# Row maxima and row scales of seven blocks moved from TensorE transposes to 32 by 32 VectorE transposes

## The reference

```python
scale = cond @ norm_w.T + 1.0
ms = jnp.mean(x * x, axis=-1, keepdims=True)
h = x * (scale[:, None, :] * jax.lax.rsqrt(ms + EPS))
u = h @ up_w.T
val, gate = jnp.split(u, 2, axis=-1)
h = val * jax.nn.gelu(gate, approximate=False)
# act_quant: s = 127 / clip(max|h| over the row, 1e-5); round(h * s) / s
# weight_quant: s = 1 / clip(mean|w|, 1e-5); clip(round(w * s), -1, 1) / s
y = act_quant(h) @ weight_quant(down_w).T
return y + x
```

## Time and profile before

| | |
|---|---|
| median of 3 runs | 760.05 us (759.47 to 760.5) |
| profiled execution, own time | 759.19 us |
| its span, first to last instruction | 757.4 us |
| TensorE matmul busy | 737.0 us, 97% |
| VectorE busy | 546.7 us, 72%, 1066 instructions |
| ScalarE busy | 345.7 us, 46% |
| GpSimd busy | 98.9 us, 13%, all in the first third |
| TensorE clock granted | 0.999 |

### The profile page before, as it was taken

How to read it: one execution, slowest core, us unless ns; L and a number is a source line. 1 busy time by engine, 2 the same in 40 slices (tenths; PEclk the granted TensorE clock), 3 DMA queues, 4 the chain that set the end, 5 groups by cost and what they waited for, 6 DMA issues and landing times.

```text
span 757.4 us, 15715 instructions
## 1 busy us (share of the span) xinstructions
PE 737.0 (97%) x6218; PEld 610.5 (81%) x6218; DVE 546.7 (72%) x1066; ACT 345.7 (46%) x674; POOL 98.9 (13%) x137
## 2 busy tenths in 40 slices
PE   3999999999999999999999999999999999999998
PEld 2888889888578887888778887788878887688864
DVE  5467777888788775878667775777758776377747
ACT  5789756443254432553235442444325342233425
POOL 2211376763413000000000000000000000000000
PEclk9999999999999999999999999999999999999999
DMA  9877673756645444343533434343443333453302
GB/s 324 285 259 241 189 264 123 229 178 223 200 135 183 153 153 148 116 140 99 183 117 116 130 116 163 108 152 122 125 160 103 98 98 117 128 170 98 103 29 84
DMA packets 43929, 116.63 MB, mean 154 GB/s; under 512 B 4944, under 2 KB 5200, under 8 KB 42704
## 3 DMA queue, kind: packets, MB, share of 16 engines
q1 hardware_dynamic: 43856, 115.63, 47.6%
HBM read 98.83 MB, written 16.78 MB: 153 GB/s over the span
## 4 chain that ended last, share of the span: by engine, by line
PE 86%; DVE 5%; ACT 3%; issue 3%; DMA 1%; POOL 0%; SPq 0%; DVEq 0%; ACTq 0%
PE ps_v L525 16%; PE ps_v L526 15%; PE ps_v L527 15%; PE ps_y L626 12%; PE ps_g L526 8%; PE ps_g L525 8%; PE ps_g L527 8%; PE ps_v L690 1%; DMA sums<-in_up_t_dram 1%; DMA h<-in_x_rows_dram 1%; ACT g L733 1%; ACT w_hi L776 1%; DVE h L1053 0%; PE ps_m L609 0%; DVE xt L1004 0%
## 5 line engine op out<-in xcount | busy, mean ns | idle before, releaser
L525 PE MATMUL ps_v<-x_hi,w_hi 128*128 128x256 f16 x1216 | 332.0, 273 | 3.3 <-DVE ps_g L1036 1.3
L527 PE MATMUL ps_v<-x_hi,w_lo 128*128 128x256 f16 x1216 | 331.9, 273 | 0.0
L526 PE MATMUL ps_v<-x_lo,w_hi 128*128 128x256 f16 x1216 | 331.9, 273 | 0.0
L526 PE MATMUL ps_g<-x_lo,w_hi 128*128 128x256 f16 x640 | 174.8, 273 | 0.0
L527 PE MATMUL ps_g<-x_hi,w_lo 128*128 128x256 f16 x640 | 174.8, 273 | 0.0
L525 PE MATMUL ps_g<-x_hi,w_hi 128*128 128x256 f16 x640 | 174.8, 273 | 0.0
L715 ACT COPY ps_g<-ps_v 128x256 f32<-128x256 f32 x96 | 34.3, 357 | 230.7 <-PE ps_v L527 230.7
L525 PEld LDWEIGHTS ps_v<-x_hi,w_hi 128*128 128x128 f16 x1216 | 119.1, 98 | 21.4 <-DVE ps_g L1036 2.7
L526 PEld LDWEIGHTS ps_v<-x_lo,w_hi 128*128 128x128 f16 x1216 | 119.1, 98 | 15.7
L527 PEld LDWEIGHTS ps_v<-x_hi,w_lo 128*128 128x128 f16 x1216 | 119.1, 98 | 13.9
L726 ACT ACTIVATE g<-ps_g,w_unscale 128x512 f32<-128x512 f32 x128 | 87.3, 682 | 68.1 <-PE ps_g L527 68.0
(11 more groups left out here) (113 smaller groups left out, 581.7 us busy)
## 6 DMA issues: line engine op xcount, KB each, us to landing
w_lo<-w_lo_dram SPq DMA_DIRECT2D x96, 448.0 KB, 3.3
q<-in_up_t_dram SPq DMA_DIRECT2D x16, 512.0 KB, 5.1
xt<-in_x_cols_dram SPq DMA_DIRECT2D x8, 1024.0 KB, 5.2
res<-in_x_rows_dram SPq DMA_DIRECT2D x26, 256.0 KB, 3.6
out_dram<-res SPq DMA_DIRECT2D x26, 256.0 KB, 2.9
sums<-in_up_t_dram SPq DMA_DIRECT2D x12, 512.0 KB, 4.7
xs<-in_x_rows_dram SPq DMA_DIRECT2D x22, 256.0 KB, 3.8
w_lo_dram<-w_lo SPq DMA_DIRECT2D x16, 256.0 KB, 4.8
```

The costliest lines, as they stand in the source:

```text
L525: pe.matmul(to, w_hi[:, wh:wh + P], hi, start=start and kt == 0, stop=False, skip_group_check=True)
L526: pe.matmul(to, w_hi[:, wh:wh + P], lo, start=False, stop=False, skip_group_check=True)
L527: last = pe.matmul(to, w_lo[:, wl:wl + P], hi, start=False, stop=(kt == 1), skip_group_check=True)
```

## The change

For blocks 0 to 6 the two groups of TensorE transposes are gone. At j = 1, after the norms, VectorE turns `h_max` in 32 by 32 squares into `ta` and reduces each group of 32 elements: each of the four groups of 32 partitions (quadrants) then holds its own part of the maxima. At j = 2, after `peak_of`, three small copies bring these to quadrant 0, where the maximum, the clamp, the reciprocal and the scale are computed on 32 partitions x 16 elements; three copies spread the scales to the other quadrants and a second 32 by 32 transposition of a broadcast view writes them into `ps_m`. `row_dequant` takes four instructions, one a quadrant. The last block keeps the old way. Buffers of the new steps lie in `ta` and `tb`, so that `difference` and the late loads have waits for them.

```diff
+Q = 32
+        turned = ta[:].rearrange("p a n -> p (a n)")
+        peak_rows = tb[:, 0, 0:TB // Q * TT].rearrange("p (k t) -> p k t", k=TT)
+        row_inv = tb[0:Q, 1, 0:TB // Q]
+        scale_all = tb[:, 1, TB // Q:2 * (TB // Q)]
+        row_peak = sb("row_peak", [P, TB // Q], F32)
...
 # SyncE, j == 4 of the last block
                         sp.wait_ge(x_lo_ready, made_before(NB))
+                        sp.wait_ge(scale_rows, NB - 1)
...
 # TensorE
             def spread_scale(b):
-                pe.wait_ge(scale_ready, b + 1)
+                pe.wait_ge(scale_ready, 1)
...
-                if 1 <= b and j == 2:
-                    spread_scale(b - 1)
...
-                if 1 <= b and j == 1:
-                    turn_max(b - 1)
...
 # VectorE, difference(c, k)
                 if k == XT1:
                     dve.wait_ge(xn_ready, c * KT + 2)
+                    dve.wait_ge(peak_step, (c - 2) * PEAK_STEPS + 1)
...
                     dve.wait_ge(t_ready, before + 1)
+                    dve.wait_ge(scale_rows, c - 1)
...
+            def turn_peaks(b):
+                dve.wait_ge(h_max_ready, (b + 1) * J)
+                dve.wait_ge(x_hi_ready, made_before(b + 1))
+                dve.wait_ge(x_lo_ready, made_before(b + 1))
+                dve.transpose(turned, h_max[:]).then_inc(max_rows, 1)
+                dve.wait_ge(max_rows, b + 1)
+                dve.tensor_reduce(peak_rows[:, 0, :], turned.rearrange("p (t n) -> p t n", n=Q), AX.X,
+                                  ALU.max).then_inc(peak_step, 1)
+
+            def spread_peaks(b):
+                base = b * PEAK_STEPS
+                dve.wait_ge(peak_step, base + 1)
+                for k in range(1, TT):
+                    dve.tensor_copy(peak_rows[0:Q, k, :], peak_rows[k * Q:(k + 1) * Q, 0, :]).then_inc(peak_step, 1)
+                dve.wait_ge(peak_step, base + 4)
+                dve.wait_ge(dequant_ready, b * TT)
+                dve.tensor_reduce(row_peak[0:Q, :], peak_rows[0:Q].rearrange("p k t -> p t k"), AX.X,
+                                  ALU.max).then_inc(peak_step, 1)
+                dve.wait_ge(peak_step, base + 5)
+                dve.tensor_scalar(row_peak[0:Q, :], row_peak[0:Q, :], CLIP, None, ALU.max).then_inc(peak_step, 1)
+                dve.wait_ge(peak_step, base + 6)
+                dve.reciprocal(row_inv, row_peak[0:Q, :]).then_inc(peak_step, 1)
+                dve.wait_ge(peak_step, base + 7)
+                dve.wait_ge(scale_rows, b)
+                dve.tensor_scalar(scale_all[0:Q, :], row_inv, QMAX, None, ALU.mult).then_inc(peak_step, 1)
+                dve.wait_ge(peak_step, base + 8)
+                for k in range(1, TT):
+                    dve.tensor_copy(scale_all[k * Q:(k + 1) * Q, :], scale_all[0:Q, :]).then_inc(peak_step, 1)
+                dve.wait_ge(peak_step, base + 11)
+                dve.wait_ge(xn_ready, min(b + 3, NB) * KT)
+                dve.wait_ge(scaled_ready, b * J)
+                dve.transpose(ps_m[:], scale_all.unsqueeze(2).to_broadcast([P, TB // Q, Q])).then_inc(scale_rows, 1)
...
 # row_dequant(b), blocks 0 to 6
+                    for k in range(TT):
+                        dve.tensor_scalar(dequant[k * Q:(k + 1) * Q, b % 2, :],
+                                          row_peak[0:Q, :].rearrange("p (i k) -> p k i", k=TT)[:, k, :], 1.0 / QMAX,
+                                          d_mean[0:Q, :], ALU.mult, ALU.mult).then_inc(dequant_ready, 1)
...
 # the order in VectorE's iteration n
-                if 1 <= b < NB and j == 2:
-                    row_scales(b - 1)
...
                 if n >= 2:
                     peak_of(n - 2)
+                if 1 <= b < NB and j == 2:
+                    spread_peaks(b - 1)
                 if b >= 2 and j < 4 and n < NJ:
                     residual(b - 2, j, ps_y[:, j % 2, :])
...
                         for kt in range(KT):
                             norm(b + 1, kt)
+                if 1 <= b < NB and j == 1:
+                    turn_peaks(b - 1)
+                if 1 <= b < NB - 1:
                     if j == 2:
                         difference(b + 1, XT1)
                         difference(b + 1, XT2)
```

More of the change, by code:

```diff
@@ L189, in bass_cond_norm_geglu_bitlinear @@
         rs_t = sb("rs_t", [P, TT], F32)
-        row_max = sb("row_max", [P, TT], F32)
-        row_rec = sb("row_rec", [P, TT], F32)
-        row_scale = sb("row_scale", [P, TT], F32)
         dequant = sb("dequant", [P, 2, TT], F32)
+        row_peak = sb("row_peak", [P, TB // Q], F32)
+        row_max = row_peak[:, 0:TT]
+        row_rec = row_peak[:, TT:2 * TT]
+        row_scale = row_peak[:, 2 * TT:3 * TT]
         d_sums = sb("d_sums", [P, ND], F32)
@@ L275, in bass_cond_norm_geglu_bitlinear @@
         row_step = sem("row_step")
+        peak_step = sem("peak_step")
         scale_ready = sem("scale_ready")
@@ L286, in bass_cond_norm_geglu_bitlinear @@
         RS_STEPS = 11
+        PEAK_STEPS = 11
         def spread_rs_at(c):
@@ L1068, in row_scales @@
             def row_scales(b):
                 dve.wait_ge(max_rows, b + 1)
-                dve.tensor_reduce(row_max[:], ps_m[:].rearrange("p (i n) -> p i n", i=TT), AX.X,
+                dve.tensor_reduce(row_max, ps_m[:].rearrange("p (i n) -> p i n", i=TT), AX.X,
                                   ALU.max).then_inc(row_step, 1)
-                dve.wait_ge(row_step, 3 * b + 1)
-                dve.tensor_scalar(row_max[:], row_max[:], CLIP, None, ALU.max).then_inc(row_step, 1)
-                dve.wait_ge(row_step, 3 * b + 2)
@@ L1075, in row_scales @@
-                dve.reciprocal(row_rec[:], row_max[:]).then_inc(row_step, 1)
-                dve.wait_ge(row_step, 3 * b + 3)
-                dve.tensor_scalar(row_scale[:], row_rec[:], QMAX, None, ALU.mult).then_inc(scale_ready, 1)
+                dve.wait_ge(row_step, 1)
+                dve.tensor_scalar(row_max, row_max, CLIP, None, ALU.max).then_inc(row_step, 1)
+                dve.wait_ge(row_step, 2)
+                dve.reciprocal(row_rec, row_max).then_inc(row_step, 1)
+                dve.wait_ge(row_step, 3)
@@ L1079, in row_dequant @@
+                dve.tensor_scalar(row_scale, row_rec, QMAX, None, ALU.mult).then_inc(scale_ready, 1)
             def row_dequant(b):
@@ L1081, in row_dequant @@
                     dve.wait_ge(d_step, 5)
-                dve.tensor_scalar(dequant[:, b % 2, :], row_max[:], 1.0 / QMAX, d_mean[:], ALU.mult,
-                                  ALU.mult).then_inc(dequant_ready, 1)
+                if b == NB - 1:
+                    dve.tensor_scalar(dequant[:, b % 2, :], row_max, 1.0 / QMAX, d_mean[:], ALU.mult,
+                                      ALU.mult).then_inc(dequant_ready, 1)
+                else:
+                    for k in range(TT):
+                        dve.tensor_scalar(dequant[k * Q:(k + 1) * Q, b % 2, :],
+                                          row_peak[0:Q, :].rearrange("p (i k) -> p k i", k=TT)[:, k, :], 1.0 / QMAX,
+                                          d_mean[0:Q, :], ALU.mult, ALU.mult).then_inc(dequant_ready, 1)
             def scaled(b, j):
@@ L1101, in residual @@
                 dve.wait_ge(y_ready, u + 1)
-                dve.wait_ge(dequant_ready, b + 1)
+                dve.wait_ge(dequant_ready, (b + 1) * TT if b < NB - 1 else b * TT + 1)
                 if late >= 0:
```

## The result

The changed kernel takes 766.13 us (median of 6 runs, 765.36 to 766.53), the kernel before 760.27 (6 runs, 759.47 to 761.12): ratio 1.0080, 95% interval 1.0069 to 1.0091. The change costs 5.9 us, where I had forecast 1.9.

What follows compares the result with a forecast made beforehand. TensorE was taken to bound the kernel (86% of the chain that ended last). Block 2's +0.37 and +0.58, blocks 3 to 6's +1.8 and block 7's -0.87 summed to +1.9 us: 761.9 us, range 759.3 to 766.0.

Steps and rivals of the forecast that it cites:

- the term of block 1: Block 1 gains 0.87 us from the removed transposes, of which 0.7 was let arrive in block 2.
- TensorE's transposes: A block's two groups of four transposes cost TensorE 0.87 us; seven blocks lose them, 6.1 us.
- j = 1 costs nothing: VectorE's first transposition and reduction, 1.35 us at j = 1, are covered by 1.49 us of idle in blocks 2 to 6.
- Blocks 3 to 6, +0.45 each: In iteration 3 TensorE's third waits for VectorE's late seed; net +0.45 us a block, +1.8 for four.
- S: Length of VectorE's eleven small steps and second transposition at j = 2: 2.58 us if copies overlap, 3.06 if not, 2.8 taken.
- S - 2.35: Net us a block in blocks 3 to 6: TensorE waits S - 1.48 ahead of third, the block gains 0.87.
- Rival 1: Every copy between quadrants is held, none overlapping: +3.4 us, 763.4 us; chance 0.25.
- Block 7, -0.87: Block 7 has no differences, so second_val waits for TensorE as before and the 0.87 us is kept.
- Block 2, +0.37 and +0.58: Block 2: hidden of iteration 33 comes 0.37 us later; row_dequant's four instructions at j = 5 add 0.58 us.
- Rival 2: VectorE's transposition runs at half speed, 1.2 us in place of 0.69: +3.2 on the sum, 765.1 us; chance 0.12.
- Rival 3: Small steps disappear in VectorE's idle time and the kernel gets faster, 752.6 us if TensorE never waits; chance 0.15.

Runs made afterwards that it cites:

- spaced2: Changed kernel with new scales only for blocks 2 to 6, row_dequant at j = 14, some ScalarE casts and VectorE differences and low parts later: 754.88 us, 0.9939.
- nocopy: Changed kernel without its six copies between quadrants, so the scales differ from the reference's: 757.50 us, 0.9965 against the kernel before.
- only0: Changed kernel with only block 0's scales made the new way, blocks 1 to 6 the old way: 763.02 us, 1.0043 against the kernel before.
- dummy1: Kernel before with three more small instructions behind row_dequant in block 1 alone: 761.89 us, 1.0037.
- small_sums: Changed kernel with GpSimd's weight sums cut to one element each: 760.95 us; its pair, the kernel before with the same cut: 757.84 us.
- dummy36: Kernel before with three more small instructions behind row_dequant in blocks 3 to 6: 759.75 us, 1.0004.
- old0: Changed kernel with block 0's scales made the old way over TensorE, blocks 1 to 6 new: 763.30 us, 1.0048 against the kernel before.
- from2: Changed kernel with the new way only for the scales of blocks 2 to 6: 761.21 us, 1.0024 against the kernel before.
- deq14: Changed kernel with all of row_dequant moved from j = 5 to j = 14: 762.88 us, 1.0043 against the kernel before.

## Why the prediction was wrong

The sign was right and the size was not: 1.9 forecast, 5.9 measured, 766.13 us where the range ended at 766.0. The step that failed is the term of block 1. By its steps:

- **TensorE's transposes, 0.87 us a block**: right. spaced2, nocopy and block 7 each show 0.87.
- **j = 1 costs nothing**: right in blocks 3 to 6. There the `h_max` copy starts 6.29 us after the norms, at 396.90, and in the kernel before 6.90. The 0.61 earlier is what the prediction had (390.95 in place of 391.56).
- **Blocks 3 to 6, +0.45 each**: the mechanism and the place right (`third` of iteration 3 waits for the seed), the size low. S was 3.01, not 2.8: net +0.64 measured, S - 2.35 gives 0.66. That is 0.8 us more in all. The formula puts all the waiting at the seed; 0.23 us of 1.50 stood at `fourth`, behind `second_val`. I had taken the middle between copies that overlap and copies that wait; all 42 waited for the one before. The Trainium skill, "VectorE: DVE Perf Modes", section "Two Vector instructions with no wait between them", says so for copies that begin in different groups of 32 partitions, and the trace agrees (a step of 0.20 each). Rival 1 thus held, but its 3.4 us are not 5.9 either.
- **Block 7, -0.87**: right.
- **Block 1, "gains 0.87, of which I let 0.7 arrive"**: the step that failed. I gave the new `row_dequant` a price in block 2 and a cover in blocks 3 to 7, and none in block 1. Four instructions took 3.10 us there, since GpSimd's weight sums run in the same stretch, and block 1 grew by 2.99 us in place of shrinking by 0.87: 3.9 of the 4.9 us by which the traces exceed the forecast. only0 (+3.2 us) and dummy1 (+2.5 from three instructions) show the loss, the pair small_sums (-0.87 in block 1) that it is GpSimd, dummy36 that in blocks 3 to 6 it is nothing. The one old row factor of block 1, 0.69 us where block 2's takes 0.22, would have told it in advance.
- **Block 2, +0.37 and +0.58**: near in size, not in its path. Block 2 grew by 2.09 us where the prediction had 1.82, and by 1.92 with GpSimd's sums cut. The wait at j = 5 went from 0.86 to 1.26 us, +0.40 for the forecast +0.58. But the longest wait there, 2.24 us, is for ScalarE's copies, whose queue holds the cast of a late difference. The prediction's formula has no ScalarE queue in it, nor a stretch at the lower clock behind the wait. That its sum comes out so near is partly luck.
- **Rival 2's counter-argument**, that all 512-element operations of 4 bytes cost one rate, does not hold: the copy into `h_max` takes 0.43 us where a reduction takes 0.69. Its conclusion, 0.69 for the transposition, was right all the same.

The prices of separate runs are 3.2 (block 0's scales, only0), 1.6 (block 1's, old0 less from2) and 1.9 (those of blocks 2 to 6, from2). Their sum, 6.7 us, is above the 5.9 of the change; the interval of each is 0.8 to 1.0 us to either side, and in the traces the prices nearly add up: blocks 1 and 2 together grew by 2.77 us in only0, by 2.08 in old0 and by 5.08 in the changed kernel. How much of block 2's loss goes through ScalarE's queue, how much through VectorE's and how much through the clock stays open.

Rival 3, the gain, failed for this change. The gain exists (spaced2), though not for the rival's reason: the steps do not vanish by being short; they have to be given a place.

## What to carry to other kernels

Price a small instruction in every stretch where it runs, not in one: read one like it from the row of that stretch, and look at what the neighbouring engine does there. When work goes from the bound engine to one that feeds it, write down that engine's slack at the place and every queue that waits for it, ScalarE's as well as TensorE's; if the slack is short, first move what isn't urgent out of the way, and then the same edit may pay (1.0080 for seven blocks became 0.9939 for the five whose surroundings had been cleared). And a half-known price of many small steps is better tested with its upper bound than with the middle.

## What the runs showed of the hardware

- An instruction of VectorE on 32 x 4 float32 numbers in SBUF takes 0.22 us alone and 0.68 to 0.78 beside GpSimd's 128 x 256 sums, and alternates with them. The Trainium skill, "SBUF — State Buffer", section "Who interferes with whom", says that the two share one pair of ports, and that where a VectorE instruction uses it in a two-port mode, the engine that issues first holds the pair for its whole instruction. The trace agrees in that the two alternate, and with the sums cut to one element the time is 0.22 again (a mean of 218 ns over all 28). Which property of this instruction asks for the shared port no run here tells.
- Earlier in block 1, beside GpSimd's work on the down weights, three 32 x 16 copies took 1.25 and 0.96 us and not the 0.55 and 0.56 of block 4. VectorE's timeline there:

```profile
114.78 1.25 DVE L1095 COPY tb<-tb 32x16 f32<-32x16 f32 x3
...
117.55 0.96 DVE L1109 COPY tb<-tb 32x16 f32<-32x16 f32 x3
```

  and GpSimd's:

```profile
114.34 0.96 POOL L907 TENSOR_SCALAR sums<-sums,d_scale 128x512 f32<-128x512 f32 x1 [1.58 <-DMA sums<-in_down_t_dram]
115.39 0.61 POOL L909 TENSOR_SCALAR sums<-sums 128x512 f32<-128x512 f32 x1
```

- A 32 by 32 transposition of 128 x 512 float32 takes 0.70 us from SBUF to SBUF and 0.73 from a broadcast view into PSUM, as much as a reduction or a two-input operation of 512 float32 elements here (0.68 to 0.75); the copy of 512 takes 0.43.
- In block 2, behind a wait of TensorE of 2.24 us, the granted clock was 0.53 for 3.6 us and the matmuls of 256 columns took 0.42 us and not 0.27. The run old0 shows the same (0.53) behind a wait of 1.99 us in that place. In deq14 and small_sums it stayed at 1.00 there, and so it did in the changed kernel behind the wait of 2.28 us in block 1. What decides it no run here tells.
